# Transposes of a block's rows moved ahead of its predecessor's first product; late routing steps, openings and gathers spread over more slots

## The reference

```python
x = x + tanh(g_xattn[0]) * attention(layernorm(x), ctx, ctx, Wq, Wk, Wv, Wo, bq, bk, bv, bo)
x = x + tanh(g_ffn[0]) * ffn(layernorm(x))

def ffn(x):                                     # top 2 of 8 experts
    probs = softmax(einsum('btd,de->bte', x, Wg))
    top_w, top_i = top_k(probs, 2)
    top_w = top_w / (sum(top_w) + 1e-8)
    combine = sum(one_hot(top_i) * top_w[..., None])
    h = square(relu(einsum('td,edh->teh', xt, W1)))
    y = einsum('teh,ehd->ted', h, W2)
    return einsum('te,ted->td', combine, y)
```

## Time and profile before

| | us |
|---|---|
| median of 3 runs | 578.19 (576.28 to 579.0) |
| the profiled execution, its own time | 576.49 |
| its span, first to last instruction | 574.7 |
| PE busy in the span | 520.9 (91%) |
| DVE, ACT, POOL busy | 366.7, 277.8, 241.8 |

### The profile page before, as it was taken

How to read it: one execution, slowest core, us unless ns; L and a number is a source line. 1 busy time by engine, 2 the same in 40 slices (tenths; PEclk the granted TensorE clock), 3 DMA queues, 4 the chain that set the end, 5 groups by cost and what they waited for, 6 DMA issues and landing times.

```text
span 574.7 us, 13340 instructions
## 1 busy us (share of the span) xinstructions
PE 520.9 (91%) x4126; PEld 471.0 (82%) x4126; DVE 366.7 (64%) x937; ACT 277.8 (48%) x564; POOL 241.8 (42%) x346
## 2 busy tenths in 40 slices
PE   4599999998999999999997969999999999999970
PEld 3498899897998898898886858999999888898960
DVE  5556567677786859977575765544456666656452
ACT  3355555555545355564454425555555454455530
POOL 5165443875678554555325320000025454322252
PEclk9999999999999999999999979999999999999996
DMA  7102213424422342354435564222236776754343
GB/s 244 62 1 80 69 56 102 138 82 150 142 68 92 113 159 93 120 165 150 155 110 176 156 215 133 79 80 74 74 93 189 209 210 201 209 161 149 119 151 115
DMA packets 63874, 73.93 MB, mean 129 GB/s; under 512 B 8128, under 2 KB 56512, under 8 KB 63808
## 3 DMA queue, kind: packets, MB, share of 16 engines
q1 hardware_dynamic: 56560, 55.45, 30.7%
q0 software_dynamic: 6272, 16.79, 9.5%
q10 hardware_dynamic: 976, 0.84, 0.5%
HBM read 42.78 MB, written 32.37 MB: 131 GB/s over the span
## 4 chain that ended last, share of the span: by engine, by line
PE 72%; DVE 12%; issue 8%; ACT 3%; another core or an unknown queue 2%; POOL 1%; DMA 0%; POOLq 0%; DVEq 0%; ACTq 0%
PE pair L945 36%; PE pair L1149 10%; PE pair L1031 8%; PE pair L982 4%; PE pair L1166 3%; PE pair L1151 2%; PE pair L1013 2%; PE pair L1207 2%; DVE hsq L1343 1%; PE pair L1062 1%; DVE xgTlo L1347 1%; PE pair L1104 1%; PE pair L1043 1%; DVE xs L1419 1%
## 5 line engine op out<-in xcount | busy, mean ns | idle before, releaser
L716 POOL DMA_INDIRECT ys<-y_scratch,list_at x64 | 61.1, 955 | 170.8 <-ACT hThi L806 118.9
L945 PE MATMUL pair<-w2hi,hThi 128*128 x284 | 85.7, 302 | 4.8 <-ACT y_sb L799 3.1
L1333 DVE TENSOR_TENSOR hTlo<-pair,hThi 128x512 fp32r<-128x512 f32 x71 | 49.0, 691 | 52.5 <-ACT hThi L806 47.0
L945 PE MATMUL pair<-w2lo,hThi 128*128 x284 | 81.1, 286 | 0.0
L703 POOL DMA_INDIRECT xe_scratch<-stage,list_at x64 | 65.5, 1024 | 35.3 <-issue 9.6
L945 PE MATMUL pair<-w2hi,hTlo 128*128 x284 | 80.0, 282 | 0.0
L1343 DVE TENSOR_TENSOR hsq<-pair,hrelu 128x512 f32<-128x512 f32 x71 | 49.0, 690 | 48.4 <-ACT hrelu L812 38.1
L945 PE MATMUL pair<-w1hi,xgThi 128*128 x142 | 63.0, 444 | 13.1 <-DVE xgTlo L1347 13.1
L812 ACT ACTIVATE hrelu<-pair 128x512 f32<-128x512 f32 x71 | 42.5, 599 | 66.8 <-PE pair L945 59.3
L1149 PE MATMUL pair<-long,probT 128*128 128x136 f32 x512 | 73.0, 285 | 0.6 <-ACT probT L885 0.6
L1149 PEld LDWEIGHTS pair<-long,probT 128*128 128x128 f32 x512 | 63.8, 190 | 4.3 <-ACT probT L885 3.6
(11 more groups left out here) (184 smaller groups left out, 1272.4 us busy)
## 6 DMA issues: line engine op xcount, KB each, us to landing
xg<-xe_scratch SPq DMA_DIRECT2D x71, 128.0 KB
y_scratch<-y_sb SPq DMA_DIRECT2D x71, 128.0 KB
raw<-in_L_ffn_W SPq DMA_DIRECT2D x16, 512.0 KB
xs<-in_x SPq DMA_DIRECT2D x16, 256.0 KB, 3.4
x_scratch<-xs SPq DMA_DIRECT2D x16, 256.0 KB, 2.2
xn_scratch<-xn SPq DMA_DIRECT2D x16, 256.0 KB
stage<-xn_scratch SPq DMA_DIRECT2D x32, 128.0 KB
x1s<-x_scratch SPq DMA_DIRECT2D x32, 128.0 KB
```

The costliest lines, as they stand in the source:

```text
L716: pool.indirect_dma_start(ys[t % YB][:, k, :].bitcast(I32), None, y_dram[:, :], bass.IndirectOffsetOnAxis(ap=list_at[:, k, t:t + 1], axis= ...
L945: mm = pe.matmul(dst, l(k), r(k), start=(k == 0 and i == 0), stop=(k == n - 1 and i == 2))
L1333: dve.tensor_tensor(hTlo[j % 2][:, :, :].rearrange("p c n -> p (c n)"), bank[2 + j % 2][:, :], hThi[j % 2][:, :, :].rearrange("p c n -> p ...
```

## The change

It has five parts.

1. In `ffn(j)` on PE, ACT and DVE the work for the rows of block j+3 (transposes, xgThi, xgTlo) stands before the first product of block j+2, hrelu and hsq.
2. The value product of the attention (slots 7, 11, 23, 27, 39 and 43) stands behind the long scores of its slot.
3. The last routing group takes a slot for each of its steps, its stores are in slots 75 and 76, and the second table starts at slot 75 and takes a step a slot up to 80. GpSimd's late stores wait for one step more.
4. Groups from tile 16 on open blocks in halves: "mid", "open0", "opened0" before "count", "open1", "opened1" behind. `sum_after` falls for the first half of such a group's tiles.
5. Every second tile's second gather is put half a step later, so a pair of tiles takes 2.5 steps and not 2. The last gathers inside the steps wait for y_sb.

```diff
-LAST_LAG = [0, 0, 1, 2, 2, 3]
-STORE_LAG = [4, 2]
+LAST_LAG = [0, 1, 2, 3, 4, 5]
+STORE_LAG = [4, 4]
-TABLE = [47, 73]
-TABLE_LAG = [[0, 1, 2, 3, 4, 5], [0, 0, 1, 1, 2, 3]]
+TABLE = [47, 75]
+TABLE_LAG = [[0, 1, 2, 3, 4, 5], [0, 1, 2, 3, 4, 5]]
@@ def sum_after(t):
-            known = t + 1 if t0 + n == NT else t0 + n
+            known = t0 + n // 2 if t0 >= FULL_AT and t < t0 + n // 2 else t0 + n
@@ def plan_gathers():
-                    last = at_half[t, k] = max(last + 1, 2 * (sum_after(t) + 2), 2 * free)
+                    last = at_half[t, k] = max(last + 1 + (k and t % 2), 2 * (sum_after(t) + 2), 2 * free)
@@ def route_names(r, lag):
-            if r == len(GROUPS) - 1:
+            if GROUPS[r][0] >= FULL_AT:
                 return [None, None, "place", "mid", "open0", "opened0", "count", "placed", "at", "open1", "opened1"]
             return [None, None, "place", "count", "placed", "at", "open0"] + ["opened0"] * (r > 0)
@@ def store_rows(r, t, k, s):
-                j = ffn_at(s) if s > FFN + 2 else None
+                j = ffn_at(s) + 1 if s > FFN + 2 else None
@@ def gather_y(t, k, half):
+                if NJ - 2 <= j < NJ and late:
+                    pool.wait_ge(a_y, j)
@@ tensor, def ffn(j):  (ACT and DVE alike)
                     mm.then_inc(t_hT, 1)
+                i = j + 3
+                if i < NJ:
+                    pe.wait_ge(d_xg[i % XG], 16 * (i // XG + 1))
+                    if i >= 1:
+                        pe.wait_ge(v_xgT, i)
+                    if i == 0:
+                        pe.wait_ge(v_max, UNITS)
+                    if i == 2:
+                        pe.wait_ge(a_exp, UNITS // GT)
+                    for c in range(DC):
+                        mm = pe.transpose(xg_bank(i)[:, c * P:(c + 1) * P], xg[i % XG][:, c * P:(c + 1) * P], ident)
+                    mm.then_inc(t_xgT, 1)
                 i = j + 2
                 if 0 <= i < NJ:
...
                     mm.then_inc(t_h, 1)
-                i = j + 3
-                if i < NJ:
...
@@ tensor, for s in SLOTS:
-                nv = value_step(s)
-                if nv is not None and s > 0:
-                    value_product(nv)
                 vs = score_half(s)
...
                     mm.then_inc(t_long, 1)
+                nv = value_step(s)
+                if nv is not None and s > 0:
+                    value_product(nv)
@@ tensor, the count:
-                    if r == len(GROUPS) - 1:
-                        mm = pe.matmul(dst[:, n + 1, :], counters[:, 1, :], both[:, 0, :], start=True, stop=True)
+                    if GROUPS[r][0] >= FULL_AT:
+                        for i in range(n // 2):
+                            mm = pe.matmul(dst[:, n + 1, :], counters[:, 1, :], both[:, i, :], start=(i == 0),
+                                           stop=(i == n // 2 - 1))
```

More of the change, by code:

```diff
@@ L807, in ffn @@
                                    ACT.Copy).then_inc(a_hT, 1)
[L808 to L812, removed]
                 i = j + 3
@@ L822, in ffn @@
                                    ACT.Copy).then_inc(a_xgT, 1)
+                i = j + 2
+                if 0 <= i < NJ:
+                    act.wait_ge(t_h, i + 1)
+                    act.wait_ge(v_hsq, i)
+                    act.activation(hrelu[:, :], bank[i % 2][:, :], ACT.Relu).then_inc(a_relu, 1)
             for s in SLOTS:
@@ L1293, in route_step @@
                 if kind == "open":
-                    known = ends if g == len(GROUPS) - 1 and i == 0 else count
+                    known = ends if t0 >= FULL_AT and i == 0 else count
                     return dve.tensor_tensor((open_ if g else opened)[:, :].rearrange("p (e m) -> p e m", m=TPE),
@@ L1335, in ffn @@
                                       ALU.subtract).then_inc(v_hT, 1)
+                i = j + 3
+                if i < NJ:
+                    dve.wait_ge(a_xgT, i + 1)
+                    dve.tensor_tensor(xgTlo[i % 2][:, :, :].rearrange("p c n -> p (c n)"), xg_bank(i)[:, 0:D],
+                                      xgThi[i % 2][:, :, :].rearrange("p c n -> p (c n)").bitcast(F32),
+                                      ALU.subtract).then_inc(v_xgT, 1)
                 i = j + 2
@@ L1343, in ffn @@
                     dve.tensor_tensor(hsq[i % 2][:, :], bank[i % 2][:, :], hrelu[:, :], ALU.mult).then_inc(v_hsq, 1)
[L1344 to L1349, removed]
                 if j in sum_at:
```

## The result

The changed kernel takes 561.06 us (median of 4 runs, 560.96 to 561.42), the kernel before took 578.6 beside it (576.28 to 582.88): ratio 0.969, 95% interval 0.9633 to 0.9747. The forecast was 566.9, with a range of 559 to 574.8, so the measured time lies near the lower edge. The sum behind the forecast was 11.3 us less, and the two profiled executions are 15.4 apart.

What follows compares the result with a forecast made beforehand. PE, busy 91% of the span, was taken as the bound, its waits as the loss. Terms -4.5 - 2.9 + 0.9 - 6.2 - 3.3 + 4.7 = -11.3 us gave 565.2, scaled 566.9; range 559 to 574.8.

Steps and rivals of the forecast that it cites:

- the pile: Slot 73: 6.75 us of routing and table steps on DVE before xgTlo; spreading them over slots was forecast at -6.2 us.
- Reading of before: From 448 to 550, 27 steps take 101.1 us where 94.0 would do: 7.1 us lost, 4.84 us of PE idle.
- Rows first, -4.5 in the gather stretch: From 448 on, xgTlo gets 1.5 us of slack instead of 0.14, so short PE waits go: -4.5 us.
- The tail is left as it is: 0: From 550 on: last gathers stay at the same steps, bound by the last y block, so 0 us.
- no shelter: Rival: late signals, late gathers or long DVE sums hold PE despite the order; -4.5 and -3.3 fall away, 574.7 us; chance 0.12.
- Overlap -2.9, block 2 +0.9: From 275 to 345, xgTlo waits outside slot 73 shrink, -2.9 us; block 2's transposes wait for the last exponential, +0.9.
- the pile only moves: Rival: DVE falls behind in slots 74 and 75 or rows come late; the 6.2 becomes 0, 573.1 us; chance 0.07.
- Value product, -3.3: Attention: six PE waits for the residual sum, 3.8 us together, go behind long scores of 1.26 us: -3.3 us.
- Halves, +4.7: Slots 50, 58 and 66: extra DVE openings before count make PE wait, longest in slot 50 beside GpSimd's xs: +4.7 us.
- Gathers, 0: Same 64 gathers spaced evenly, 2.5 steps a pair, last ones at the same steps: 0 us.
- late-rows rival: Rival "Slower": rows 0.5 us late in each of 37 steps stop PE's transposes, +18.5 us, 585.4 us; chance 0.05.
- The signs: Expected in the changed profile: count waits of 1 to 3.5 us in slots 50, 58, 66; 27 steps in 96 to 98 us.

Runs made afterwards that it cites:

- on record: The two profiled executions, kernel before and changed kernel, that the prediction was about; medians beside them 578.6 and 561.06 us.
- set 2: Four kernels on a chip of its own, the kernel before and the changed kernel rerun unchanged among them: 565.06 and 561.06 us, ratio 0.9934.
- whole openings with bursts: Changed kernel without part 4 and without the gather spacing of part 5: 557.36 us, ratio 0.9635 to the kernel before.
- halves only: Kernel before with part 4 alone, openings in halves and sum_after with them: 584.46 us, ratio 1.0086.
- Rows first alone: Kernel before with part 1 alone, rows of block j+3 first in a step: 563.63 us, ratio 0.9964.
- Whole openings: Changed kernel with part 4 undone, whole groups opened at once as before: 555.5 us, ratio 0.9821 to the kernel before.
- xs behind stores: Changed kernel with GpSimd's bias added to xs behind the stores in slot 50: 561.57 us, ratio 0.9702 to the kernel before.
- count first: Changed kernel, halves kept, with step count directly behind mid, ahead of open0 and opened0: 556.36 us, ratio 0.9842 to the kernel before.

## Why the prediction came out as it did

The time and the sign were right. Three terms came out near their forecasts for the reasons given: the pile, the value product, and the waits of the halves. The rest is luck in part. The gains of rows first rest on a loss that comes and goes with the chip: where signals aren't late, the whole change is worth 3.7 us, a third of the 11.3 forecast. And misses of both signs offset each other, -3.70 at the tail and -0.84 between blocks 15 and 40 against +1.7 at the halves and +0.8 at the value product. Step by step:

- *Reading of before.* "7.1 us are lost" from 448 on is right for the execution on record and others like it. It is no property of the kernel: on the chip of set 2 its 27 steps take 94.04 us with no change at all, though all sums and bursts are in place, and PE waits for nothing between 448 and 545. So a tile's sums, which the prediction named beside a late hrelu, cost nothing. The four waits for xgTlo there on record (0.66, 0.56, 1.25 and 0.63 us) stand behind three hrelu and one xgThi that came 0.88 to 1.54 us late. The 2% forecast, and the 3.1% measured, hold where signals come late; elsewhere the change is worth 0.7%.
- *Rows first, -4.5 in the gather stretch:* -4.74 measured, and between 15 and 40 another -0.84 that I had at nothing. On a quiet chip, one without late signals, -0.5, and that is a shorter step, 3.465 us for 3.483.
- *"The tail is left as it is: 0":* the step that failed by most, -3.70. On a quiet chip the tail differs by 0.6. The rest is late signals that met the old order's last blocks, and no term of the sum took that up. The last y_sb, before on record and before in set 2:

```profile
563.67 0.38 ACT L799 ACTIVATE y_sb<-pair 128x256 f32<-128x256 f32 x1 [4.79 <-remote]
```

```profile
552.92 0.38 ACT L799 ACTIVATE y_sb<-pair 128x256 f32<-128x256 f32 x1 [1.94 <-PE pair L945]
```

No part of the change is shown to shelter these blocks: whole openings with bursts, in the new order, waits 3.15, 2.56 and 3.17 us before its last three y_sb and ends in 28.50, while halves only, in the old order, ends in 24.99.
- *The rival "no shelter"* fell. Its point, that 7.1 us were lost and only 4.84 idle, isn't settled by the runs; that late signals are behind it fits, for on the quiet chip both the loss and the idle time are gone (94.04 us, and 0.44 idle of 102).
- *Overlap -2.9, block 2 +0.9:* over-sized. Rows first alone gives +0.60 up to hThi 0, where the predicted wait for the last exponential falls (0.82 us), and -0.91 between blocks 0 and 9, in sum -0.3 for a forecast of -2.0. The waits for xgTlo outside the pile do shrink, from 3.74 to 2.03 us, but only about half of that reaches the steps. On record the second piece was -2.50, and that is luck: 2.65 us at 314.68 were a wait for a late y_sb, 0.53 in the changed kernel; in set 2 the piece is -0.84.
- *Last group and table, -6.2:* -6.62 on record and -6.6 alone, 5.9 of it between the cuts of set 2, where before had the shorter half clock. PE's longest wait between 330 and 345 is 0.55, the clock stays full, no block's rows were late. The rival "the pile only moves" fell.
- *Value product, -3.3:* -2.5 alone. I missed the 0.5 given back.
- *Halves, +4.7:* the mechanism was right, place and cause: waits of 3.00, 1.35 and 0.80 where there were 0.37, 0.38 and none, the longest in slot 50 and held by GpSimd. That is 4.4 us idle. Of clock the sum held nothing, although it had priced that very effect at the pile; (1 - 0.77) x 15 + (1 - 0.83) x 10 makes 5.1 us behind the first two waits. But only 6.4 remain in the table (5.4 + 1.0), so the clock is worth some 2 us and not 5. From the twelfth attnThi to the thirteenth, with slot 50, the kernel before takes 18.21 us in set 2 and the changed one 21.78; from the fourteenth to the fifteenth, with slot 58, 15.15 and 17.08. Whole openings has a half clock too, 0.51 from 226.8 to 230.2, and takes 18.25 in the first: there the half clock costs nothing, and two waits that stand behind it elsewhere (0.24 for logits, 0.30 for xnTlo) are gone.
- *Gathers, 0:* 1.2 to 1.5 us slower at the end. The late-rows rival fell: behind the start no transfer stands among the releasers of PE's waits.
- *The signs.* Two of those named came out otherwise: the wait in slot 66 is 0.80 and not 1 or more, and the 27 steps take 94.0 us and not 96 to 98. The chances given, with the 0.04 more, add up to 1.04; the three classes add up to 1.

Terms by the parts alone, on quiet chips: -2.0, -2.5, -6.6; with +6.4 and the tail's +1.3 less 1.3, near -4.7 against a measured -3.7.

## What to carry to other kernels

Before a term is built on lost time, look whether each late start has a releaser; time that the profile puts down to nothing it can name may be the chip's, and the same kernel can measure 2.5% apart on two chips. Slack in the instruction order is worth little on a quiet chip and a good deal on one with late signals. Where a step must be added ahead of a signal that PE waits for, put it behind the signal: one swap of names here gave 4.7 us back, where undoing the whole part gave 5.6. And a stretch of half clock priced by its length is an upper bound: in the attention phase waits behind it gave way.

## What the runs showed of the hardware

- The kernel before takes 578 to 580 us in two measurements and 565 in two others, on other chips, with the changed kernel at 561 in both kinds. In the first kind the traces also hold fewer records of signals: 7,267 for the kernel before against 9,636. Why signals come late there stays open.
- DVE's instructions with two inputs in SBUF last until GpSimd's two-input add has ended: open 1.98 and 1.55, placed 2.02, against 0.42 and 0.23 free; which one is held follows where xs is put. Placed ends 0.09 us behind the end of xs each time and open 0.29. DVE's instructions that read PSUM at the same time keep their length (the attention's 128x256 product 0.42, top 0.79, count 0.17). The held instruction is not always the later one: placed began 0.63 us before the start recorded for xs in xs behind stores, and would have been done in 0.23. Whether the add begins before its recorded start, the traces don't show. The Trainium skill (GPSIMD Engine Reference, Key points) has this contention, and these runs agree with it.
- The clock fell for 3.4 us behind PE waits of only 0.37 to 0.52: in slot 50 with whole openings, in slots 50 and 58 with count first. It did not behind the 0.38 of slot 58 with whole openings, nor behind the same 0.37 in the kernel before or with the value product alone moved. What decides it stays open.
